# Carrying the scan's state into the second half by one-column products on TensorE, in two of three decay buffers

## What is computed

```python
x = x + mamba(group_norm(x), ...)          # state-space scan along the 1024 pixels
x = x + linear_attention(group_norm(x), ...)
```

```python
def step(h, inp):                          # L = 1024 steps, 512 channels x 16 states
    dt_t, B_t, C_t, x_t = inp
    dA = jnp.exp(dt_t[..., None] * A)
    h = dA * h + (dt_t * x_t)[..., None] * B_t[:, None, :]
    y = jnp.einsum('bdn,bn->bd', h, C_t)
```

## Time and profile before

| what | value |
|---|---|
| median of 3 runs | 665.24 us (664.08 to 667.45) |
| profiled execution: its own time | 671.67 us |
| profiled execution: span of the trace | 669.9 us, granted clock 0.987 |
| scan stage | 119.6 to 448.6 us, granted clock 1.00 |
| busy share of the span | PE 92%, DVE 79%, ACT 57%, POOL 55% |

### The profile page before, as it was taken

The page is one execution under the profiler, slowest core; times in us unless marked ns, Lnnn a source line. Parts: engine busy times, 40 slices in busy tenths (PEclk is TensorE's granted clock), DMA queues, the critical chain, the costliest instruction groups (busy, mean ns, idle before and its releaser), DMA issues.

```text
span 669.9 us, 25303 instructions
## 1 busy us (share of the span) xinstructions
PE 618.6 (92%) x11404; PEld 438.1 (65%) x11404; DVE 530.5 (79%) x546; ACT 381.3 (57%) x743; POOL 368.6 (55%) x164
## 2 busy tenths in 40 slices
PE   2999999899978999999999999999799699999997
PEld 1443445789967788877888779888655455555533
DVE  5795612899979999998878999996978697992465
ACT  1774785987866777778666777621155345333100
POOL 1000504599988898899988899990400044533000
PEclk9998999999999999999999999999799799999999
DMA  6990645200363201522430100016059899790203
GB/s 224 75 82 6 170 139 170 63 20 20 75 146 88 67 20 41 139 50 83 113 97 20 51 19 21 3 36 196 1 114 187 174 243 211 179 176 0 59 7 125
DMA packets 72626, 62.11 MB, mean 93 GB/s; under 512 B 34024, under 2 KB 57576, under 8 KB 72520
## 3 DMA queue, kind: packets, MB, share of 16 engines
q1 hardware_dynamic: 71560, 60.09, 40.6%
q10 hardware_dynamic: 960, 0.41, 0.2%
HBM read 44.22 MB, written 15.25 MB: 89 GB/s over the span
## 4 chain that ended last, share of the span: by engine, by line
PE 80%; DVE 6%; DMA 6%; ACT 4%; issue 3%; SPq 1%; DVEq 0%; ACTq 0%
PE PS L1119 34%; PE PS L1138 8%; PE PS L1001 7%; PE PS L1253 7%; DMA patch_rows<-arena 5%; PE PS L1344 4%; PE PS L1166 4%; PE PS L1359 4%; PE PS L1135 2%; PE PS L972 1%; PE PS L1232 1%; SPq L483 1%; PE PS L1330 1%; PE PS L1010 1%; PE PS L1028 1%
## 5 line engine op out<-in xcount | busy, mean ns | idle before, releaser
L558 POOL TENSOR_TENSOR X<-X,spare 128x2048 f32<-128x2048 f32 x32 | 146.9, 4590 | 10.0 <-DVE X L1576 8.6
L1119 PE MATMUL PS<-mid,arena 128*32 128x128 f32 x4096 | 133.2, 273 | 8.6 <-issue 7.3
L1119 PE MATMUL PS<-WPR,arena 128*32 128x128 f32 x2048 | 127.5, 273 | 8.1 <-DVE X L1580 2.9
L1119 PEld LDWEIGHTS PS<-mid,arena 128*32 128x32 f32 x4096 | 118.2, 110 | 25.3 <-issue 19.2
L1119 PEld LDWEIGHTS PS<-WPR,arena 128*32 128x32 f32 x2048 | 112.7, 110 | 24.4 <-issue 14.4
L1119 PE MATMUL PS<-APROD,arena 128*32 128x128 f32 x2048 | 126.1, 274 | 1.2 <-issue 0.9
L788 ACT ACTIVATE arena<-arena,small 128x512 f32<-128x512 f32 (+1 forms) x150 | 99.5, 713 | 34.7 <-DVE X L1580 11.5
L1119 PEld LDWEIGHTS PS<-APROD,arena 128*32 128x32 f32 x2048 | 109.7, 110 | 2.7 <-issue 2.4
L583 POOL TENSOR_TENSOR arena<-arena,PWR 128x512 f32<-128x512 f32 x30 | 40.6, 1383 | 72.7 <-PE PS L1253 72.6
L558 POOL TENSOR_TENSOR arena<-arena,spare 128x2048 f32<-128x2048 f32 x16 | 73.3, 4583 | 6.0 <-DVE arena L1576 5.4
L558 POOL TENSOR_TENSOR WIN<-WIN,spare 128x2048 f32<-128x2048 f32 x16 | 73.4, 4586 | 3.7 <-DVE WIN L1576 2.7
(11 more groups left out here) (192 smaller groups left out, 1060.0 us busy)
## 6 DMA issues: line engine op xcount, KB each, us to landing
arena<-dt_rows SPq DMA_DIRECT2D x56, 256.0 KB, 4.1
arena<-patch_rows SPq DMA_DIRECT2D x40, 324.0 KB, 6.2
patch_rows<-arena SPq DMA_DIRECT2D x10, 648.0 KB, 7.5
X<-in_x SPq DMA_DIRECT2D x4, 1024.0 KB, 7.5
dt_rows<-arena SPq DMA_DIRECT2D x8, 512.0 KB, 3.2
spare<-c_rows SPq DMA_DIRECT2D x64, 64.0 KB, 2.2
tap_rows<-WPR SPq DMA_DIRECT2D x24, 88.0 KB, 8.6
mid<-dt_rows SPq DMA_DIRECT2D x8, 256.0 KB, 3.5
```

Source lines behind the costliest of these rows:

```text
L558: pool.tensor_tensor(HB[s % 4], HB[s % 4], CROW[:, k % 2:k % 2 + 1, :].broadcast_to([P, QN, HALF]), ALU.mult).then_inc(S["g_rd"], 1)
L1119: mm = pe.matmul(PS[32 * n:32 * n + 32, 4 + i, j * P:(j + 1) * P], DXT[:, DT_ * b + g, 4 * h + j, 32 * i:32 * i + 32], DIAGB[k % 2][n][:, ...
```

## The change

In a second half, only the pairs with q % 3 == 0 are still scanned tile by tile (`by_tile`): 22 of the 64 pairs. The 42 others are one scan of 1024 columns, as in a first half. The first tile's carried state is the scan's start value. The second tile's carried state can't be, so it is put into the input: h at the first column should be decay*carry + input. VectorE makes decay*carry for the second tile of each pair, `CARRYD`, once for a quarter in steps 6, 10, 14, 18 of each image (`carry`, 8 small products in all). TensorE adds it to column 0 of the second tile in PSUM: four products of one column (identity x CARRYD), one for each group of 32 partitions.

For that the decay at pixel 512 is needed early: VectorE copies that column of dt to `DTMAX` (`middle_column`, 2 copies), ScalarE takes its exponent with all rates (`half_way`, 8 activations of 16 columns, ahead of `diagonals(1, 2)`), and `late_by_four` moves these with the rates (48 columns where 16 were). Decay buffers 1 and 2 keep their zero at column 512 throughout, so ScalarE skips that column there in second halves too, and only one memset of three is left. Two waits on `top_rd` become waits on `col_rd`.

```diff
@@ -103,6 +103,7 @@
         CARRY = view(mid, 19200, B * DT_, NQ, QN)
+        CARRYD = view(mid, 19328, B * DT_, NQ, 2)
@@ -147,9 +148,9 @@
         RATES = view(small, 256, DT_, NS)
-        RATES1 = view(small, 320, DT_, NS)
+        LATE = small[:, 320:512].rearrange("p (k g n) -> p k g n", k=3, g=DT_)
         RATEQ = view(small, 512, QN, DT_, NQ)
-        RATEQ1 = view(small, 576, QN, DT_, NQ)
+        LATEQ = small[:, 576:768].rearrange("p (i k g q) -> p i k g q", i=QN, k=3, g=DT_)
         SELQ = sb("SELQ", [P, 2, 32])
@@ -335,14 +336,18 @@
+        def by_tile(q):
...
+            return step_of(q // 2)[1] == 1 and q % 3 == 0
...
         def dt(e):
...
         def rates_of(b):
-            return RATES1 if b else RATES
+            return LATE[:, 0] if b else RATES
         def rates_at(b):
-            return RATEQ1 if b else RATEQ
+            return LATEQ[:, :, 0] if b else RATEQ
@@ -420,7 +425,7 @@
                 sp.wait_ge(S["dx_rd"], 2 * g + 2)
-                sp.wait_ge(S["top_rd"], NG)
+                sp.wait_ge(S["col_rd"], 2)
                 first_dt(g)
@@ -700,12 +705,18 @@
                     act.wait_ge(dt_st[e - DT_], 16)
-                    act.wait_ge(S["top_rd"], DT_)
+                    act.wait_ge(S["col_rd"], 1)
                 act.activation(DXT[:, e].rearrange("p j c -> p (j c)"), tile_pair("tr", e), ACT.Copy).then_inc(S["dxt_rd"], 1)
-            def take_late_rates():
+            def half_way(e):
+                b, g = divmod(e, DT_)
+                act.wait_ge(S["rate_rd"], b + 1)
+                act.wait_ge(S["col_rd"], b + 1)
+                act.activation(LATE[:, 1 + b, g, :], rates_of(b)[:, g, :], ACT.Exp, scale=DTMAX[:, e:e + 1]).then_inc(S["a0_rd"], 1)
...
+            def take_halves():
                 act.wait_ge(S["quad_ps"], 2)
-                act.activation(RATEQ1.rearrange("p i g q -> p (i g q)"), bank(pair_of("halves", 0), 0)[:, 0:QN * NS], ACT.Copy).then_inc(S["quad_rd"], 1)
+                act.activation(LATEQ.rearrange("p i k g q -> p (i k g q)"), bank(pair_of("halves", 0), 0)[:, 0:3 * QN * NS], ACT.Copy).then_inc(S["quad_rd"], 1)
@@ -784,7 +795,7 @@
                 for i in (2 * p, 2 * p + 1):
-                    at, first = (i - 2 * p) * HALF, 0 if h else i % 2
+                    at, first = (i - 2 * p) * HALF, 0 if by_tile(q) else i % 2
                     act.activation(DECAY[q % 3][:, at + first:at + HALF], DTR[2 * b + h][g][:, i, first:HALF], ACT.Exp,
@@ -796,6 +807,8 @@
             decay(5)
+            for e in range(NG):
+                half_way(e)
             diagonals(1, 2)
@@ -806,7 +819,7 @@
                 if s == DT_:
-                    take_late_rates()
+                    take_halves()
                 if k + 1 < STEPS // DT_:
@@ -1045,14 +1058,14 @@
-            def late_rates_by_four():
+            def late_by_four():
                 pe.wait_ge(*freed("halves", 0))
-                pe.wait_ge(S["rate_rd"], B)
+                pe.wait_ge(S["a0_rd"], NG)
                 for i in range(QN):
                     for n in range(QN):
-                        to = bank(pair_of("halves", 0), 0)[32 * n:32 * n + 32, NS * i:NS * i + NS].rearrange("p (g n) -> p g n", g=DT_)
-                        mm = pe.matmul(to, IDENT[:, 32 * i:32 * i + 32], RATES1.rearrange("p g (q n) -> p g n q", n=QN)[:, :, n, :], start=True, stop=True)
+                        to = bank(pair_of("halves", 0), 0)[32 * n:32 * n + 32, 48 * i:48 * i + 48].rearrange("p (g n) -> p g n", n=QN)
+                        mm = pe.matmul(to, IDENT[:, 32 * i:32 * i + 32], LATE.rearrange("p k g (q n) -> p (k g) n q", n=QN)[:, :, n, :], start=True, stop=True)
                 mm.then_inc(S["quad_ps"], 1)
@@ -1113,11 +1126,17 @@
                     pe.wait_ge(S["scan_rd"], q - 1)
+                carried = h and not by_tile(q)
+                if carried:
+                    pe.wait_ge(S["carry_rd"], NQ * b + nq + 1)
                 for i in (2 * p, 2 * p + 1):
...
                             mm = pe.matmul(PS[32 * n:32 * n + 32, 4 + i, j * P:(j + 1) * P], DXT[:, DT_ * b + g, 4 * h + j, 32 * i:32 * i + 32],
-                                           DIAGB[k % 2][n][:, j, :], start=True, stop=True)
+                                           DIAGB[k % 2][n][:, j, :], start=True, stop=not (carried and j == 0 and i % 2))
+                        if carried and j == 0 and i % 2:
+                            for n in range(QN):
+                                pe.matmul(PS[32 * n:32 * n + 32, 4 + i, 0:1], IDENT[:, 32 * n:32 * n + 32], CARRYD[:, DT_ * b + g, nq, i // 2:i // 2 + 1], start=False, stop=True)
                 mm.then_inc(S["u_ps"], 1)
@@ -1151,7 +1170,7 @@
                     if s == DT_ and c == 0:
-                        late_rates_by_four()
+                        late_by_four()
                     if s >= 3 - c:
@@ -1542,20 +1561,28 @@
             convolve(5)
+            def middle_column(b):
...
+                dve.wait_ge(S["rate_rd"], b + 1)
+                dve.tensor_copy(DTMAX[:, DT_ * b:DT_ * b + DT_], DTS[b][:, :, HALF]).then_inc(S["col_rd"], 1)
...
             convolve(6)
...
             rates(0)
+            middle_column(0)
             for e in range(DT_, NG):
...
             rates(1)
+            middle_column(1)
             dve.memset(arena[:, 18432:20480].rearrange("p (k l) -> p k l", l=2 * HALF)[:, :, HALF:HALF + 1], 0.0).then_inc(S["zero_rd"], 1)
...
                 q = 2 * s + p
+                start = CARRY[:, DT_ * b + g, nq, 2 * p:2 * p + 1] if h else 0.0
                 if p == 0 and s >= 4:
@@ -1571,18 +1598,21 @@
                     dve.wait_ge(S["kept"], NQ * DT_ * b + DT_ * nq + g + 1)
-                    first, second = (CARRY[:, DT_ * b + g, nq, 2 * p + r:2 * p + r + 1] for r in range(2))
-                    dve.tensor_tensor_scan(HB[s % 4][:, 2 * p, :], DECAY[q % 3][:, 0:HALF], bank(2 + p, 0), first, ALU.mult, ALU.add)
+                if by_tile(q):
+                    second = CARRY[:, DT_ * b + g, nq, 2 * p + 1:2 * p + 2]
+                    dve.tensor_tensor_scan(HB[s % 4][:, 2 * p, :], DECAY[q % 3][:, 0:HALF], bank(2 + p, 0), start, ALU.mult, ALU.add)
                     dve.tensor_tensor_scan(HB[s % 4][:, 2 * p + 1, :], DECAY[q % 3][:, HALF:], bank(2 + p, 1), second, ALU.mult, ALU.add).then_inc(S["scan_rd"], 1)
                 else:
-                    if b and p + 2 * nq * DT_ + 2 * g < 3:
-                        dve.wait_ge(S["zero_again"], p + 2 * g + 1)
-                    dve.tensor_tensor_scan(HB[s % 4][:, 2 * p:2 * p + 2, :].rearrange("p g l -> p (g l)"), DECAY[q % 3], pair(2 + p), 0.0, ALU.mult, ALU.add).then_inc(S["scan_rd"], 1)
...
-            def clear_first(q):
...
-                dve.wait_ge(S["scan_rd"], q - 2)
-                dve.memset(DECAY[q % 3][:, HALF:HALF + 1], 0.0).then_inc(S["zero_again"], 1)
+                    if q == STEPS + 2:
+                        dve.wait_ge(S["zero_again"], 1)
+                    dve.tensor_tensor_scan(HB[s % 4][:, 2 * p:2 * p + 2, :].rearrange("p g l -> p (g l)"), DECAY[q % 3], pair(2 + p), start, ALU.mult, ALU.add).then_inc(S["scan_rd"], 1)
...
+            def carry(b, nq):
...
+                heads = slice(DT_ * b, DT_ * b + DT_)
+                dve.wait_ge(S["quad_rd"], 2)
+                dve.wait_ge(S["kept"], NQ * DT_ * b + DT_ * nq + DT_)
+                dve.tensor_tensor(CARRYD[:, heads, nq, :], CARRY[:, heads, nq, 1::2], LATEQ[:, 1::2, 1 + b, :, nq].rearrange("p i g -> p g i"), ALU.mult).then_inc(S["carry_rd"], 1)
@@ -1593,13 +1623,13 @@
                 scan(s, 0)
-                if s == STEPS // 2 - 1:
-                    clear_first(STEPS)
-                elif s == STEPS // 2:
-                    clear_first(STEPS + 2)
+                if s == STEPS // 2:
+                    dve.wait_ge(S["scan_rd"], STEPS)
+                    dve.memset(DECAY[0][:, HALF:HALF + 1], 0.0).then_inc(S["zero_again"], 1)
                 scan(s, 1)
-                if s == STEPS // 2 - 1:
-                    clear_first(STEPS + 1)
+                b, h, nq, _g = step_of(s - 3)
+                if s >= 3 and h == 0 and s % DT_ == 2:
+                    carry(b, nq)
                 if s >= 3 and step_of(s - 3)[2] == NQ - 1:
```

More of the change, by code:

```diff
@@ L289, in mamba_attention_kernel @@
             ln_mu_ps ln_cent ln_sq ln_var_ps ln_lnv ln_rstd ln_mul ln_aff ln_out
-            diagd_rd kept a_exp a_rd lim_inv rate_rd quad_ps quad_rd xi_ps c0_rd c1_self c1_rd xc_rd zi_ps sz_rd
-            xd_ps xd_rd bt_ps bt_rd v_ps dt_rd top_rd dx_rd dxt_ps dxt_rd
-            zero_rd zero_d zero_again diagb_rd da_rd u_ps scan_rd g_rd y_ps y_rd
+            diagd_rd kept col_rd a_exp a_rd lim_inv rate_rd quad_ps quad_rd xi_ps c0_rd c1_self c1_rd xc_rd zi_ps sz_rd
+            xd_ps xd_rd bt_ps bt_rd v_ps dt_rd top_rd dx_rd dxt_ps dxt_rd a0_rd
+            zero_rd zero_d zero_again diagb_rd da_rd u_ps scan_rd carry_rd g_rd y_ps y_rd
```

## The result

| kernel | median | runs | ratio to the kernel before, 95% interval |
|---|---|---|---|
| before | 664.95 us | 664.08 to 667.45 (6) | 1 |
| after | 670.35 us | 666.58 to 672.11 (6) | 1.0062 [1.0033, 1.0091] |

By the ratio the change costs 4.1 us (2.2 to 6.1); the medians lie 5.4 apart. The forecast was 663.6; the measured median lies outside the range of 659.0 to 670.0 too, by 0.35 us.

The account below looks back on a forecast made before the run. Second halves were taken as bound by TensorE in eight heavy steps and VectorE in eight light ones. Heavy +0.2, light -2.2 and start +0.4 gave -1.6 us, a median of 663.6 us, range 659.0 to 670.0.

Parts of the forecast that it names:

- one-column products and their cover: TensorE, 42 second-half pairs: four added products cost 0.13 us a pair, 5.5 us of its time, mostly hidden.
- light steps: Eight steps per second half without the x*D part on TensorE; VectorE sets their time; forecast -2.2 us together.
- mutual waiting: Heavy steps: TensorE and VectorE wait for each other for 1.7 us a half, which should mostly go.
- Heavy steps: Eight steps per second half with the x*D part, TensorE's 4.79 us just above VectorE's 4.72; forecast +0.1 us a half.
- my own sum with that rule: Heavy steps: eight instructions at about 25 ns cost 0.20 us a pair, 1.5 us more, making the forecast no change.
- the floor: Heavy steps: TensorE's shortest possible step of 4.79 us, at least 38.3 us for eight, before the added products.
- The merge: VectorE, second halves: 42 pairs go from 2.36 to 2.20 us as single scans, 6.7 us of its time.
- The start: Start of the scan stage: eight ScalarE activations, 1.0 to 1.8 us, delay step 4's diagonals; +0.4 us (0 to 1.4).
- At nothing: Parts booked at no cost, among them column copies, `col_rd` waits, wider rate products and six first-half carry products.
- Scans that set all steps: Rival: VectorE's scans set every second-half step, so all 42 merged pairs count; -5.9 us, 659.3 us; chance 0.30.
- The drain: Rival: added products wait for their just-written column, 0.40 us a pair; 670.9 us; chance 0.17, including products dear in another way.
- TensorE's instruction supply: Rival: 672 more instructions, 7%, lengthen some 18 us of TensorE's issue waits by 1.3 us; 664.9 us; chance 0.05.

Follow-up runs that it names:

- e1: The changed kernel without its 42 x 4 one-column products, all else kept (second tiles' carried state left out): 663.97 us, ratio 0.9989.
- e8: The changed kernel with the eight early activations replaced by two VectorE products and one activation of 128 columns: 671.08 us, ratio 1.0086.
- e2: The kernel before plus only the change's preparations; second-half pairs all scanned tile by tile, no one-column products: 666.00 us, ratio 1.0028.
- e12: The changed kernel with ScalarE adding the carry in PSUM instead of TensorE, second tile made first, all 64 pairs merged: 663.36 us, ratio 0.9975.
- e5: The changed kernel with the four one-column products ahead of the block that overwrites their columns, not adding: 668.55 us, ratio 1.0060.
- e10: The changed kernel with identity and carry of the one-column products in bfloat16, one instruction each instead of two: 669.68 us, ratio 1.0074.
- e4: The changed kernel with each four one-column products replaced by one using the whole 128-column identity: 675.12 us, ratio 1.0170.

## Why the prediction was wrong

*The failing step is that of the one-column products and their cover.* I priced them at 42 x 0.13 = 5.5 us of TensorE's time, and let most of it vanish: hidden under VectorE and GpSimd in the light steps, and in the heavy ones under the mutual waiting. The size was nearly right, since they cost 4.9 to 6.7 us of the kernel's time, but by luck: their own time is 42 x 0.07 = 2.9 us, and the rest is TensorE waiting for instructions, which the sum left out. The cover was wrong. Light steps: from e1 to after they grew by 2.45 us where I had booked nothing. Heavy steps: by 4.4, where I had booked 21 x 0.13 = 2.7.

*Where it was too little and where too much.* Undisturbed, the eight instructions cost 0.07 us a pair, 9 ns each, even less than the 16 ns of the earlier trace rows. The rest is idle time inside blocks (7.0 us for 3.1), which those bursts couldn't show. The Trainium skill's rule that I set aside (page "TensorE: Matmul & The Clock Gate", section "Wait — 56ns, not 53.3ns?": some 25 ns from start to start however few the columns) doesn't describe the undisturbed block. The second four products, though, cost 8.8 / 42 = 0.21 us a pair, 26 ns each, and my own sum with that rule, no change at all, would have been nearer. That is a coincidence: undisturbed the second four take 0.06 us, and the rest is pauses and what they set off.

*Mutual waiting.* I expected the 1.7 us a half above the floor to go. In e1, without products, about half of it went: 78.47 us in 16 steps with a floor of 16 x 4.79 = 76.6. With them the floor is 76.6 + 21 x 0.07 = 78.1, and the steps take 82.85; the loss is 4.7 us, more than the 3.9 of before. A TensorE that stops now and then inside a block makes VectorE late, although VectorE has less to do on average.

*The merge.* 42 x 0.16 = 6.7 us of VectorE's time was too much by the start value's price. At 0.10 it is 4.2, close to what the busy times say: 152.28 us in the second halves before, 148.76 in e1 with two carry products in them. Of this 2.6 us reached the kernel in e1.

*The start.* The activations last longer than the copy of the earlier trace rows:

```profile
127.10 1.68 ACT L715 ACTIVATE small<-small,DTMAX 128x16 f32<-128x16 f32 x8
...
128.68 1.27 ACT L731 ACTIVATE mid<-cst,mid 128x128 f32<-128x128 f32 x4
```

1.58 us to the diagonals, within the 1.0 to 1.8 forecast, and GpSimd's step 4 waits for once (its carry copy of the earlier trace rows then started at once):

```profile
143.81 0.19 POOL L560 COPY mid<-X 128x4 f32<-128x4 f32 x1 [0.53 <-DVE X L1608]
```

These 0.53 us are near the +0.4 of the sum, and e8 shows that removing the activations gives nothing measurable. The preparations as a whole cost 1.9 us (0.5 to 3.2) in e2, of which 0.4 was booked. The six `carry` products in first halves, booked at nothing with 1.3 us as their end, are candidates for the rest: in after they last 0.15 to 0.87 us each, 2.9 in all. Whether they held anything up, no kernel tests; what the rest is, if there is one, stays open.

*At nothing.* The one `carry` product of a half whose place is in the light steps took 0.15 us for the 0.2 booked. The wait for `carry_rd` never showed. And where no product stands in the block, in e1, single light steps ran nearly as forecast: 5.08 and 5.26 us with a gate from step 49 on (forecast 5.08), then 4.73 and 4.73 without (forecast 4.67). Over the 15 steps the gain was 1.0 us, not 2.2.

*The rivals.* Scans that set all steps (659.3): no, TensorE sets them in turn; even e12, with all 64 pairs merged and no added product, reached only 663.4. That every GpSimd row of the second halves waits for a scan, which spoke for it, was too strong as well: in the earlier trace rows the second of two products did not. The drain (670.9): right in time and wrong in cause, as e5 has the same price with nothing to drain. TensorE's instruction supply (664.9): right in kind, with a chance of 0.05, and undersized at +1.3 us by scaling all `issue` waits with the number of instructions, where the supply's pauses alone grew by 3.9. That gauge was wrong as well: over the whole stage the loads' waits of the earlier trace rows fell.

```profile
PEld PS L1135 <- issue: 29.5, 58, 1.9
```

Most of these are loads that wait while earlier products still run. What tells is TensorE's own idle time inside a block, 2.7 us before and 7.0 after.

*What stays open* is why some transfers of instructions start late, and why the timed runs of e10 (half the added instructions) are as slow as after, while its trace shows half of after's loss (3.5 of 6.8 us). That the added product waits for its column is excluded.

## What to carry to other kernels

TensorE used up its instructions here about as fast as they arrived, so a small instruction inside a dense block cost more than its own time: place additions ahead of a wait, where they cost nothing measurable here, or give them to an engine with 20 us to spare. Before calling a step bound by another engine, look at the idle time of this one in the middle of its blocks, and see whether the pauses stand a fixed number of instructions apart. And compare more than one execution: here the two profiled ones differed by 0.4 us, and the kernels by 4.

## What the runs showed that I had not expected

- TensorE's instructions came in transfers of 16 KB, 256 of them at a time, and each of the 204 pauses inside input blocks stood at such a border and ended 1.2 to 1.7 us behind a landing.
- A product whose weights fill all 128 output rows, amid products of 32, held up the stream by some 0.5 us (0.63 us between the loads around it, where 0.11 is usual; the block is 0.45 longer), and made e4 the dearest form of the same addition: 12 us over e1, for a quarter of the instructions.
- A scan of 1024 columns that starts from a column in SBUF takes 2.35 us, one that starts from a constant 2.28.
- An activation of 16 columns with a scale taken from SBUF: 0.29 us, against 0.22 for a copy of 64 columns.
- ScalarE's addition to one column of PSUM takes 0.24 us, and 64 of them fitted beside the decays.
